# The last three chunks of the first segment sums of a graph layer: when TensorE loads its registers, runs extra products, and makes the last chunk's terms

## What is computed

```python
feat = (h @ fc_w.T).reshape(n, heads, out_feats)          # 8 heads of 32
el = jnp.sum(feat * attn_l, axis=-1)
er = jnp.sum(feat * attn_r, axis=-1)
e = jax.nn.leaky_relu(el[src] + er[dst], 0.2)
m = jax.ops.segment_max(e, dst, num_segments=n)
ex = jnp.exp(e - m[dst])
ssum = jax.ops.segment_sum(ex, dst, num_segments=n)
rst = jax.ops.segment_sum(feat[src] * (ex / ssum[dst])[..., None], dst, num_segments=n)
```

## Time and profile before

| what | value |
|---|---|
| median of 3 runs | 2163.2 us (2162.46, 2163.2, 2171.91) |
| the profiled execution | 2164.12 us, span 2162.0 us |
| mean granted TensorE clock | 0.792 |
| rescale before chunk 10 ends, last sums of the stage end | 565.5, about 666 us |
| busy in the span | PE 70%, DVE 67%, POOL 63%, ACT 19% |

### The profile page before, as it was taken

The page is one execution under the profiler, slowest core; times in us unless marked ns, Lnnn a source line. Parts: engine busy times, 40 slices in busy tenths (PEclk is TensorE's granted clock), DMA queues, the critical chain, the costliest instruction groups (busy, mean ns, idle before and its releaser), DMA issues.

```text
span 2162.0 us, 28858 instructions
## 1 busy us (share of the span) xinstructions
PE 1510.2 (70%) x7701; PEld 1142.3 (53%) x7702; DVE 1450.5 (67%) x2290; ACT 419.2 (19%) x780; POOL 1365.3 (63%) x1396
## 2 busy tenths in 40 slices
PE   6346656656558443788666687877787787579997
PEld 4235545545446343676555444655555555368874
DVE  3357777777776787676444366677677666777766
ACT  1100000000004000100000033444444444110127
POOL 0477777777720888777777723677777777135544
PEclk9657877877779555899787889888877777689999
DMA  3654444444414665444444336999999999778821
GB/s 97 164 133 124 126 125 123 126 126 122 121 36 129 173 171 146 135 130 129 115 120 119 110 108 214 316 338 342 340 341 342 344 331 345 284 254 294 292 70 60
DMA packets 234908, 406.13 MB, mean 188 GB/s; under 512 B 33199, under 2 KB 171621, under 8 KB 228197
## 3 DMA queue, kind: packets, MB, share of 16 engines
q0 software_dynamic: 73216, 219.89, 32.9%
q1 hardware_dynamic: 161637, 185.66, 27.3%
HBM read 330.93 MB, written 74.48 MB: 188 GB/s over the span
## 4 chain that ended last, share of the span: by engine, by line
POOL 48%; PE 19%; issue 18%; DMA 6%; DVE 6%; SPq 1%; ACT 1%; DVEq 0%; ACTq 0%; POOLq 0%
POOL row_space L875 44%; PE ps L1189 9%; DMA row_space<-tab_kv,src_i 3%; PE ps L1290 3%; DMA item_v<-row_space 2%; PE ps L1399 2%; POOL base L884 2%; POOL acc L884 1%; PE ps L1419 1%; POOL arena L884 1%; PE ps L990 1%; PE ps L962 1%; PE ps L1085 1%; DMA arena<-rows_block_dst 0%; PE ps L1214 0%
## 5 line engine op out<-in xcount | busy, mean ns | idle before, releaser
L875 POOL DMA_INDIRECT row_space<-tab_feat,src_i x760 | 752.1, 990 | 300.8 <-issue 231.2
L875 POOL DMA_INDIRECT row_space<-tab_kv,src_i x416 | 393.3, 946 | 195.6 <-issue 124.3
L1189 PE MATMUL ps<-arena 128*128 128x257 f32 (+1 forms) x1664 | 420.4, 414 | 121.2 <-DVE arena L2157 114.8
L1189 PEld LDWEIGHTS ps<-arena 128*128 128x128 f32 x1664 | 338.3, 207 | 196.6 <-issue 138.7
L1290 PE MATMUL ps<-arena 128*128 128x265 f32 x768 | 241.2, 480 | 110.6 <-DVE ps L2400 47.3
L1085 PE MATMUL ps<-acc,arena 128*128 x832 | 289.3, 508 | 0.0
L2151 DVE TENSOR_TENSOR arena<-row_space,ps 128x1280 f32<-128x1280 f32 (+1 forms) x94 | 174.3, 1854 | 142.0 <-DMA row_space<-tab_feat,src_i 140.2
L1290 PEld LDWEIGHTS ps<-arena 128*128 128x128 f32 x768 | 181.2, 242 | 159.0 <-issue 117.6
L1569 ACT COPY acc<-ps 128x265 f32<-128x265 f32 (+2 forms) x75 | 28.2, 376 | 1114.7 <-PE ps L1189 542.8
L1085 PEld LDWEIGHTS ps<-acc,arena 128*128 128x128 f32 x832 | 198.0, 250 | 39.0
L1969 DVE TENSOR_TENSOR arena<-row_space,ps 128x1024 f32<-128x1024 f32 x104 | 126.8, 1219 | 134.6 <-PE ps L1085 84.8
(11 more groups left out here) (380 smaller groups left out, 2190.9 us busy)
## 6 DMA issues: line engine op xcount, KB each, us to landing
item_v<-row_space SPq DMA_DIRECT2D x52, 1024.0 KB, 8.0
row_space<-item_v SPq DMA_DIRECT2D x52, 1024.0 KB, 5.0
arena<-rows_block_dst SPq DMA_DIRECT2D x104, 128.0 KB
row_space<-tab_feat,src_i POOLq DMA_INDIRECT x760, 2.8
scores<-rows_block_dst SPq DMA_DIRECT2D x52, 128.0 KB
arena<-rows_src_low SPq DMA_DIRECT2D x52, 128.0 KB
row_space<-tab_kv,src_i POOLq DMA_INDIRECT x416
arena<-rows_type SPq DMA_DIRECT2D x52, 128.0 KB
```

The lines of the kernel that those rows point to most:

```text
L875: nc.gpsimd.indirect_dma_start(rows_of_slot(s)[:, g, :], None, table, bass.IndirectOffsetOnAxis(ap=src_i[:, item:item + 1], axis=0),).then ...
L1189: last = nc.tensor.matmul(ps[:, SUM_BANKS:2 * SUM_BANKS][:, bass.ds(bs[g], 1), 0:width].rearrange("p a d -> p (a d)"), onehot[:, s % 2, g, ...
```

## The change

On TensorE, `sums_first` first waits until the terms in TERM_BANK have been read, runs 4 unread products, loads the registers for the sums and the terms, runs 4 more, and only then waits for the rescale. In chunk 10 it makes term products 0 and 1 of chunk 12 (after group 2, and between the transposes and the lane ends); in chunk 11 only 2 and 3, after groups 0 and 1. Ahead of the shares of chunk 12 there are 11 unread products in place of 8, and 7 more behind its factors. On VectorE the reads move likewise: terms 0 and 1 to chunk 10, ahead of `lane_tops` and ahead of `stitch`; terms 2 and 3 ahead of the builds of groups 2 and 3. In chunk 11 the logits follow the last build and one set of item one-hots.

```diff
--- before.py
+++ after.py
@@ -75,7 +75,8 @@
 SHARE_BANK, IOTA_AT = 3, 256
 LAST_ONEHOT_AT = 12288
 WARM_HALF = 6
-WARM = 8
+WARM_SUMS = 8
+WARM_SHARES = 11
 RESIDUAL_BANK = 1
 BIG = 1.0e30
 PAD_DST = NP - 1
@@ -1294,22 +1295,33 @@
                         if g % QUAD == QUAD - 1:
                             last.then_inc(sum_mm, 1)
 
-                def sums_first(c, terms=False):
+                def warm(count):
+                    for _ in range(count):
+                        nc.tensor.matmul(ps[:, TERM_BANK, 0:D], ident[:], w_b[:, 0, :], start=True, stop=True)
+
+                def sums_first(c, before_last):
+
+                    pe.wait_ge(score_read[1], nth(CHUNKS - 1, 1) + 2 if before_last else nth(CHUNKS - 2, 3) + 2)
+                    warm(WARM_SUMS // 2)
+                    banks, cleared = sum_banks(c, 0)
+                    pair = term_blocks(CHUNKS - 1, 2 if before_last else 0)
+                    warm(WARM_SUMS // 2)
                     pe.wait_ge(sum_mm, c * CHUNK_COUNT + CREDIT)
                     for s in range(SLOTS):
-                        if s % 2 == 0:
-                            banks, cleared = sum_banks(c, s)
-                            if terms:
-                                pair = term_blocks(c + 1, s)
                         group_sums(c, s, banks, cleared)
-                        if terms:
-                            term_products(c + 1, s, pair)
+                        if s == 1:
+                            banks, cleared = sum_banks(c, 2)
+                        if before_last and s < 2:
+                            term_products(CHUNKS - 1, 2 + s, pair)
+                        if not before_last and s == 2:
+                            term_products(CHUNKS - 1, 0, pair)
                     transposed(c + 1)
+                    if not before_last:
+                        term_products(CHUNKS - 1, 1, pair)
                     lane_ends(c + 1)
                     carries(c + 1)
-                    if terms:
-                        for _ in range(WARM):
-                            nc.tensor.matmul(ps[:, TERM_BANK, 0:D], ident[:], w_b[:, 0, :], start=True, stop=True)
+                    if before_last:
+                        warm(WARM_SHARES)
                     shares(c + 1)
                     factors(c + 1)
 
@@ -1361,8 +1373,9 @@
                 period(0, True, False, True)
                 with nc.tensor.Fori(0, CHUNKS - 4) as u:
                     period(u + 1, False, False, True)
-                sums_first(CHUNKS - 3)
+                sums_first(CHUNKS - 3, False)
                 sums_first(CHUNKS - 2, True)
+                warm(WARM_SUMS - 1)
                 period(CHUNKS - 1, False, True)
                 pe.wait_ge(sum_mm, QUADS + TICKS + CREDIT)
                 end()
@@ -2432,24 +2445,29 @@
 
                 def sums_first(c, half, turn, last):
 
+                    end = CHUNKS - 1
                     rescale(c)
                     for g in range(1, SLOTS):
                         build(c, half, g)
-                        if last:
-                            next_terms(c + 1, 1 - half, g - 1, False)
+                        if last and g < SLOTS - 1:
+                            next_terms(end, 0, g + 1, False)
                     if last:
-                        next_terms(c + 1, 1 - half, SLOTS - 1, False)
-                        item_onehots(last_onehot[:, 0], c + 1, 0)
-                        dve.wait_ge(score_read[1], nth(c + 1, SLOTS - 1) + 2)
+                        dve.wait_ge(weighted_made, end * SLOTS)
+                        item_onehots(last_onehot[:, 0], end, 0)
+                        dve.wait_ge(score_read[1], nth(end, SLOTS - 1) + 2)
                     make_logits(c + 1, turn + half, 1 - half)
                     if last:
-                        item_onehots(last_onehot[:, 1], c + 1, 1)
+                        item_onehots(last_onehot[:, 1], end, 1)
+                    else:
+                        next_terms(end, 0, 0, False)
                     lane_tops(c + 1)
                     if last:
-                        item_onehots(last_onehot[:, 2], c + 1, 2)
+                        item_onehots(last_onehot[:, 2], end, 2)
+                    else:
+                        next_terms(end, 0, 1, False)
                     stitch(c + 1)
                     if last:
-                        item_onehots(last_onehot[:, 3], c + 1, 3)
+                        item_onehots(last_onehot[:, 3], end, 3)
                     numerators(c + 1)
                     factor_terms(c + 1)
                     build(c + 1, 1 - half, 0)
```

## The result

| | median | runs | profiled execution | span |
|---|---|---|---|---|
| before | 2165.31 us | 6 (2159.41 to 2171.91) | 2164.12 us | 2162.0 us |
| changed | 2148.86 us | 6 (2146.13 to 2160.66) | 2160.66 us | 2158.5 us |

The ratio is 0.9931, with a 95% interval of 0.9909 to 0.9953: faster by 0.69%, 14.9 us; the two medians lie 16.5 us apart. The forecast was 2149.0, in a range of 2145 to 2156.

What follows compares the result with a forecast made beforehand. Bound: a loop of VectorE rescales and builds and TensorE sums between 565 and 666 us. Gains 2.3 + 3.7 + 5.4 + 2.8 = 14.2 us took 2164.12 to about 2149.9, or 2149.0 from the median; range 2145 to 2156.

Steps and rivals of the forecast that it cites:

- chunk 10: factors to the end of group 0: Chunk 10's start: sums hardly start earlier, but group 0 runs at full clock; gain 3.1 us, bounds 1.0 and 3.8.
- chunk 10: terms: Chunk 12's term products and reads placed in chunk 10: cost 0.2 on TensorE and 0.6 ahead of the stitch.
- chunk 11: factors to the end of group 0: Chunk 11's start: sums start at 604.3, not 605.99, and group 0 takes 3.7 us; gain 3.7, bounds 1.5 and 4.2.
- chunk 11: group 0 to lane scans: With only terms 2 and 3 left in chunk 11, lane scans start at 14.0 us, not 19.4; gain 5.4, bounds 2.9 and 6.5.
- chunk 12: Extra products raise the clock, so group 0 falls from 6.56 to 3.7 us; gain 2.8, bounds -2.4 and 3.1.
- The bound: Between 565 and 666 us a loop of VectorE and TensorE sets the time; savings should reach the end.
- Rows: Last gather of the stage lands at 612.9, logits need it near 616.4: not the next wait, by 3.5 us.
- The loads beside the products: Chunks 10 and 11: register loads run while matmuls are queued, as one at 614.1 did; 36 registers take 3.5 us.
- Rival 3: Loads run after the new products, not beside: loss 4 us with rising clock, 9.5 without, 2167 to 2173; chance 0.04.
- chunk 12's seven calls: 14 products behind chunk 12's factors: 3.2 us at full clock, done at 648.3 before the sums; half clock 6.0, done 651.1.
- The chance of 0.74: Whole kernel: probability of being faster by more than 0.5%, 10.8 us; the forecast case, 2146 to 2152, had 0.71.

Runs made afterwards that it cites:

- x5: Changed kernel, but register loads of chunks 10 and 11 wait by a semaphore until the 8 products ahead of them have run: stage 100.7 us.
- x2: Kernel before plus loads ahead of the wait and all extra products, chunk 12's terms not moved: ratio 0.9944, stage 94.7 us.
- x3: Kernel before with only the register loads moved ahead of the wait, no new products, terms not moved: 2167.9 us, stage 98.9 us.
- x4: Changed kernel without the 7 calls behind chunk 12's factors: stage 91.7 us.
- x7: Changed kernel with all 8 calls of chunks 10 and 11 ahead of the register loads, none behind: stage 90.5 us.
- x9: Changed kernel with all 8 calls ahead of the loads, 14 before chunk 12's shares, 5 behind its factors: ratio 0.9920, median 2147.85 us.
- x6: Changed kernel with 14 calls before chunk 12's shares in place of 11, 5 behind its factors in place of 7: stage 90.0 us.
- x11: Changed kernel with 6 calls ahead of the loads, none behind, 14 before chunk 12's shares, 5 behind its factors, six executions: ratio 0.9916, median 2147.97 us.

## Why the prediction was right, point by point

| step | forecast | the profile after | its second profile |
|---|---|---|---|
| chunk 10: factors to the end of group 0 | 3.1 | 3.5 | 3.3 |
| chunk 10: terms | -0.8 | -1.1 | -1.3 |
| chunk 11: factors to the end of group 0 | 3.7 | 4.3 | 4.3 |
| chunk 11: group 0 to lane scans | 5.4 | 5.7 | 5.8 |
| chunk 11: scans to factors | 0 | 0.3 | 0.3 |
| chunk 12 | 2.8 | 1.5 | 2.8 |
| sum | 14.2 | 14.1 | 15.2 |

(Gains in us against the profile before.)

- The bound was right: from chunk 10's factors to the last sums the chain of waits of the profile after runs through the same two engines, but for 0.8 us of ScalarE (618.39 to 619.20). Ahead of the sums of chunks 10 and 11 it now runs through the unread products, which let the sums start 1.1 and 1.5 us after the rescale. That the stage's gain reaches the end, the times alone show: 14.9 us, with an interval of 10.2 to 19.7. Rows did not become late, but they are nearer: the last gather of this stage starts at 614.96 in the profile after, and the logits read its rows at 620.53. With 2.74 us to land, as at 528.70, 2.8 us are to spare as an estimate, where 3.5 were forecast.
- The loads beside the products were the step that carried most. The forecast rested on one row, the load at 614.1. The profile after shows it for the new loads, and where it is taken away (x5) the stage is 9 to 10 us longer.
- Rival 3's price was wrong. Its late starts (3.2, 2.8 and 4.3 us), less what the clock gives back, come to a loss of 4 us only if chunk 11's gain from the terms, 5.4, is left out.
- Chunk 11's start was under-sized (4.3 against bounds of 1.5 to 4.2). I took 1.8 to 3.4 us for the second eight products after loads that end at 602.1. All sixteen took 5.44 us, because the first eight still ran while the registers loaded and the clock rose within the second eight.
- The terms in chunk 10 cost 1.1 to 1.3 in place of 0.8. VectorE had 0.69 us of idle time ahead of the stitch; the second read and the one-hots fill it and push the stitch. Part of the cost isn't the terms'. The carries behind the stitch also ran at half clock (L1266, 0.58 us, 590.74), but so they did in x2 and x3, which move no terms and still lost 0.4 us in this stretch. In the four profiles that move the terms and have the carries at full clock (x4, x5, x7, x9; 0.38 us) the stretch lost 0.9.
- The mis-sized term is chunk 12's seven calls. "3.2 us at full clock, done at 648.3 before the sums" held in the second profile (3.27) and not in the first (4.96), nor in x7 (4.96). TensorE idled 2.1 us between the 22 products and the shares in all three. In the first the clock then fell at 638.5 among the fourteen, and they ended 1.8 us after the rescale. Where TensorE idled 1.2 us or less there (x2, x5, x6, x9 to x11), the products behind the factors ran at full clock in all six profiles. The Trainium skill says (TensorE: Matmul & The Clock Gate, section on the HAM clock gate) that the monitor isn't tied to the program, so the same kernel is cold for more or fewer matmuls from run to run. The two profiles agree: the same products took 4.96 and 3.27 us.
- The closeness of the number is luck. In the first profile the surplus of the other pieces (0.4, 0.6, 0.3 and 0.3 us) makes up for what chunk 12 (1.3) and the terms in chunk 10 (0.3) lack; the second sums to 15.2. And the median of the kernel before moved from 2163.2 with three runs to 2165.31 with six, so a time within 0.2 us of the forecast says no more than that the gain was about 15.
- The chance of 0.74 for over 0.5% rested on a forecast 3.4 us beyond that bound; the interval reaches from 0.47% to 0.91% and so over it on both sides.

## What to carry to other kernels

Load the registers for dynamic addresses ahead of the wait, not behind it; in this kernel 20 registers cost 2.15 us behind the wait and 36 cost 3.73, and beside queued matmuls the sums did not wait for them. Products to raise the clock belong in idle time that is there anyway, enough of them to leave no gap up to the work they are for. Here a set that followed 2.1 us of idle time fell to half clock in two profiles of three, and products that themselves delay the work (chunk 11) earned only 0.2 us. And when the runs scatter by about as much as the change is worth, measure the stage between two fixed events in each profile: it repeated to 0.2 and 1.1 us in the two kernels that were profiled twice, where the intervals of the times are 3 to 6 us to either side.

## What was not expected

Most of the scatter between executions is not in this stage. In the thirteen profiles the rest, from the last sums of this stage to the end, took 1491.9 to 1502.4 us, and what lies ahead, up to chunk 10's factors, 560.6 to 565.9. The stage itself took 88.5 and 88.7 us in the two profiles with six calls, and 91.35 and 90.3 in the two of the changed kernel. Part of the rest's scatter lies in the gathers of the attention block (GpSimd's row for them: min, median and longest of one in ns, first and last start), 525.7 us here in the profile after, with a rest of 1501.9:

```profile
L876 POOL DMA_INDIRECT row_space<-tab_kv,src_i x416: 941/946/1593, 1319.8 to 1845.5; - x139
```

and 521.4 in the second experiment's, with a rest of 1495.0:

```profile
L876 POOL DMA_INDIRECT row_space<-tab_kv,src_i x416: 942/948/1657, 1316.9 to 1838.3; - x139
```

What makes it longer I have not tried to find. A new wait has also appeared: group 3 of chunk 11 stands 0.94 us for ScalarE's clearing of a bank at 618.80 to 619.20, 0.2 us behind the build it needs anyway (618.96). It costs next to nothing here; whether it would be next with faster builds was not tried.
